# Tree feed-forward of an audio tower: four of eight levels weighed by ACT, residual added by GpSimd, one packed integer for four leaf numbers

## What is computed

```python
for _ in range(DEPTH + 1):                 # 8 levels, 255 nodes
    all_nodes.append(current)
    score = jnp.einsum('td,td->t', flat_x, w1s[current]) + b1s[current]
    all_logits.append(score)
    choice = ((jnp.sign(score) + 1.0) / 2.0).astype(jnp.int32)
    current = current * 2 + choice + 1
path_weights = jax.nn.gelu(jnp.abs(logits), approximate=False)
for i in range(DEPTH + 1):
    t_i = jnp.einsum('td,tdo->to', flat_x, w2s[nodes_i]) + b2s[nodes_i]
    out = out + t_i * path_weights[:, i][:, None]
...
h = h + _L0_ffn_ref(_layernorm(h, axis=-1), ...)
```

## Time and profile before

| | us |
|---|---|
| median of 3 runs (lowest to highest) | 495.93 (495.58 to 497.63) |
| the profiled execution | 497.14 |
| its span, first to last instruction | 495.4 |
| convolution, attention, sorting | 0 to 363 |
| static tiles, from the first gate | 367.6 |
| first overflow product | 420.45 |
| last product of the last overflow tile | 483.6 |
| last output DMA issued by GpSimd | 487.6 to 488.6 |

### The profile page before, as it was taken

One profiled execution on the slowest core, in us unless ns is written; L12 is line 12 of the kernel. 1 busy time (PEld: TensorE's weight loads), 2 busy tenths in 40 slices (PEclk: granted clock), 3 DMA queues, 4 the chain that ended last, 5 costly groups with the idle time before them and its releaser, 6 DMA issues.

```text
span 495.4 us, 8210 instructions
## 1 busy us (share of the span) xinstructions
PE 362.6 (73%) x2578; PEld 246.1 (50%) x2578; DVE 353.8 (71%) x619; ACT 297.0 (60%) x691; POOL 266.6 (54%) x354
## 2 busy tenths in 40 slices
PE   1158997767998897878987798834069887778880
PEld 1145665545555554456644475522057665545550
DVE  0558869897988888988889979776129999433341
ACT  1357987799789986777976658561013332544551
POOL 4324687885686846855896617417506555321111
PEclk9988989999999999898998989855569999999997
DMA  4443541339969722312441200197151220000000
GB/s 95 120 104 84 125 101 41 93 78 226 202 146 156 162 53 63 93 33 63 110 109 27 69 1 11 38 133 99 32 132 35 56 54 10 6 7 4 7 3 7
DMA packets 58424, 36.99 MB, mean 75 GB/s; under 512 B 31645, under 2 KB 57079, under 8 KB 58378
## 3 DMA queue, kind: packets, MB, share of 16 engines
q1 hardware_dynamic: 54250, 33.55, 33.6%
q0 software_dynamic: 3328, 2.36, 1.9%
q10 hardware_dynamic: 800, 0.49, 0.5%
HBM read 11.15 MB, written 7.50 MB: 38 GB/s over the span
## 4 chain that ended last, share of the span: by engine, by line
DVE 39%; PE 27%; ACT 15%; issue 11%; DMA 5%; POOL 1%; SPq 1%; DVEq 0%; POOLq 0%; ACTq 0%
DVE nm L1367 12%; ACT Z L1183 8%; PE Z L914 8%; DVE pre L1634 6%; PE Z L1051 5%; DVE va L1626 4%; DMA pre<-in_x 3%; DVE va L1396 2%; PE Z L1053 2%; ACT q L1125 2%; PE Z L1057 2%; DVE pre L1463 1%; ACT k L1125 1%; ACT va L1276 1%; PE Z L1055 1%
## 5 line engine op out<-in xcount | busy, mean ns | idle before, releaser
L1367 DVE TENSOR_REDUCE nm<-Z 125x1 f32<-125x748 f32 x192 | 175.4, 932 | 38.9 <-PE Z L914 33.2
L1183 ACT ACTIVATE Z<-Z,nm 125x748 f32<-125x748 f32 x192 | 166.1, 870 | 61.5 <-DVE nm L1367 61.2
L914 PE MATMUL Z<-pool_a 128*125 128x512 f16 (+1 forms) x768 | 164.5, 342 | 27.3 <-ACT Z L1183 23.7
L914 PEld LDWEIGHTS Z<-pool_a 128*125 128x125 f16 x768 | 88.7, 141 | 71.6 <-ACT Z L1183 45.6
L717 POOL DMA_INDIRECT out<-pre,va x44 | 42.7, 971 | 87.8 <-DVE pre L1640 78.3
L1634 DVE TENSOR_REDUCE pre<-va 128x64 f32<-128x512 f32 x44 | 45.1, 1025 | 1.3
L1276 ACT COPY va<-Z 32x520 f32<-32x520 f32 x48 | 27.9, 580 | 30.3 <-PE Z L1057 30.1
L781 PE MATMUL Z<-xhT,wq 128*128 128x249 f16 (+1 forms) x192 | 33.4, 295 | 10.5 <-DVEq L1377 9.2
L1183 ACT ACTIVATION_READ_ACCUMULATOR Z<-Z,nm 125x1 f32 x192 | 41.1, 214 | 0.0
L1051 PE MATMUL Z<-pool_a,qk 128*32 x96 | 29.6, 390 | 14.1 <-ACT va L1276 8.7
L646 POOL DMA_INDIRECT sorted_rows<-xrow,slot x24 | 30.4, 1266 | 15.3 <-DVE slot L1519 8.7
(11 more groups left out here) (237 smaller groups left out, 620.9 us busy)
## 6 DMA issues: line engine op xcount, KB each, us to landing
pool_a<-pool_a SPq DMA_DIRECT2D x64, 187.0 KB, 3.3
pool_a<-pool_a SPq DMA_DIRECT2D x64, 93.5 KB, 2.2
sorted_rows<-zrow SPq DMA_DIRECT2D x1, 3640.0 KB, 22.1
va<-sorted_rows SPq DMA_DIRECT2D x11, 260.0 KB, 3.4
w<-in_L_ffn_w2s SPq DMA_DIRECT2D x1, 2048.0 KB, 16.6
pre<-in_x SPq DMA_DIRECT2D x4, 375.0 KB
pool_a<-in_L_ffn_w2s SPq DMA_DIRECT2D x1, 1024.0 KB
out<-pre,va POOLq DMA_INDIRECT x44, 2.1
```

The source lines that it names most:

```text
L914: last = mm(z[0:XP, c0:c1], kst[:, u % 3, a, hd, KST[t]:KST[t] + XP], qst[:, u % 3, hd, c0:c1], start=(a == 0), stop=(a == 1))
L1183: sc_.activation(z, z, ACT.Exp, bias=nm[0:XP, u % 4, i:i + 1], accum_out=sm[0:XP, u % 4, i:i + 1]).then_inc(s_exp, 1)
L1367: v.tensor_reduce(nm[0:XP, u % 4, i:i + 1], Z[n % 3][0:XP, 0:N], X, ALU.max, negate=True).then_inc(s_max, 1)
```

## The change

Three edits, all in the feed-forward.

1. **Weighing.** In static tiles ACT weighs levels 0 to 3 (`AW = 4`), one instruction of 64 columns for each, with the level's gate as a scale for each row (`weigh_first`). DVE weighs levels 4 to 7 in one instruction of 256 columns. A new semaphore, "weighted_by_act", tells that ACT is done; PE's bank and DVE's sum wait for both. ACT's weighing of tile k waits until the sum of tile k - 2 has been made, since `wy` has two buffers. Overflow tiles are weighed as before.
2. **Residual.** DVE no longer adds it. GpSimd does, just ahead of the DMA in `rows_out`, for all tiles, and the DMA waits for it.
3. **Leaf numbers.** DVE packs four leaves of 7 bits in one integer (`lam4`), with two more instructions before "group_offsets". PE loads one integer a tile, after group 0 of the tile before, and for the first tile of a block ahead of the branch, so also for the blocks that are skipped. The node is cut out by one formula for all groups.

```diff
@@ def rows_out(k), GpSimd
+                pool.wait_ge(s_sl, k + 1)
+                o = yo[:, k % NO, :]
+                gp.tensor_tensor(o, o, xs[:, (k // 4) % NX, k % 4, C_H:C_ID], ALU.add).then_inc(s_yo, 1)
                 pool.wait_ge(s_yo, k + 1)
@@ def bank_ready(n), PE
                 elif n >= NY:
                     pe.wait_ge(s_wy, n - NY + 1)
+                    pe.wait_ge(s_wa, n - NY + 1)
@@ def load_leaves(k), PE
-                return [nc.tensor.value_load(lami[0:1, 2 * kk + i:2 * kk + i + 1], min_val=0,
-                                             max_val=LEAVES * LEAVES - 1) for i in range(2)]
+                return nc.tensor.value_load(lam4[0:1, kk:kk + 1], min_val=0, max_val=LEAVES ** 4 - 1)
@@ def overflow_products(k, leaves), PE
-                    if g % 2:
-                        return pairs[g // 2] >> (7 + sh)
-                    return (pairs[g // 2] >> sh) & (LEAVES - 1 >> sh)
+                    return (leaves >> (7 * g + sh)) & (LEAVES - 1 >> sh)
...
-                    if g == 2 and k % 4 < 3:
-                        following = load_leaves(k + 1)
...
+                    if g == 0 and k % 4 < 3:
+                        following = load_leaves(k + 1)
@@ blocks of overflow tiles, PE
+                leaves = load_leaves(4 * m)
                 with pe.If(groups > 4 * (4 * m - ST_TILES)):
                     xs_T(m)
-                    pairs = load_leaves(4 * m)
@@ static tiles, ACT
+            def weigh_first(k):
+
+                act.wait_ge(s_gelu, k + 1)
+                if k >= 2:
+                    act.wait_ge(s_sl, k - 1)
+                y = y_bank(k)
+                for n in range(AW):
+                    last = sc_.activation(wy[:, k % 2, n * D:(n + 1) * D], y[:, 0, n, 0:D], ACT.Copy,
+                                          scale=gw[:, k % 4, n:n + 1])
+                last.then_inc(s_wa, 1)
...
                 gates(k, y_bank(k))
+                weigh_first(k)
@@ leaf numbers, DVE
+            link(v.tensor_scalar(lam4[:], lami[:, 1::2], 14, None, ALU.logical_shift_left))
+            v.tensor_tensor(lam4[:], lam4[:], lami[:, 0::2], ALU.bitwise_or).then_inc(s_goff, 1)
@@ def weigh(k), DVE
+                y = y_bank(k)
+                v.tensor_tensor(w[:, 1], y[:, 1, :, 0:D], gv[:, 1], ALU.mult).then_inc(s_wy, 1)
@@ def sum_levels(k), DVE
+                if k < ST_TILES:
+                    dve.wait_ge(s_wa, k + 1)
...
-            def add_residual(k):
-                dve.wait_ge(s_sl, k + 1)
-                o = yo[:, k % NO, :]
-                v.tensor_tensor(o, o, xs[:, (k // 4) % NX, k % 4, C_H:C_ID], ALU.add).then_inc(s_yo, 1)
```

More of the change, by code:

```diff
@@ L163, in tower @@
         lami = sb("lami", [1, OVG // 2], i32)
+        lam4 = sb("lam4", [1, OVG // 4], i32)
         lamq = sb("lamq", [1, OVG], i32)
@@ L181, in tower @@
         NY = 3
+        AW = 4
         def y_bank(n):
@@ L214, in tower @@
             "slots", "ln2_rstd", "w1_columns")]
-        (s_b0, s_bnp, s_bn, s_bq8, s_z7, s_zl, s_abs, s_xp, s_xc, s_y, s_yv, s_wy, s_sl, s_yo) = [sem(n) for n in (
-            "b0_in", "bn_by_feature", "bn_ready", "q_bias_ready", "w7_zeros", "low_zeros", "gate_abs", "xs_T", "xsT_copied", "y_ready", "y_moved", "weighted", "levels_summed", "rows_out")]
+        (s_b0, s_bnp, s_bn, s_bq8, s_z7, s_zl, s_abs, s_xp, s_xc, s_y, s_yv, s_wa, s_wy, s_sl, s_yo) = [sem(n) for n in (
+            "b0_in", "bn_by_feature", "bn_ready", "q_bias_ready", "w7_zeros", "low_zeros", "gate_abs", "xs_T", "xsT_copied", "y_ready", "y_moved", "weighted_by_act", "weighted", "levels_summed", "rows_out")]
         vs, ps_, as_ = sem("vector_step"), sem("pool_step"), sem("scalar_step")
@@ L1029, in load_leaves, with overflow_products @@
                 kk = k - ST_TILES
-                return [nc.tensor.value_load(lami[0:1, 2 * kk + i:2 * kk + i + 1], min_val=0,
-                                             max_val=LEAVES * LEAVES - 1) for i in range(2)]
-            def overflow_products(k, pairs):
+                return nc.tensor.value_load(lam4[0:1, kk:kk + 1], min_val=0, max_val=LEAVES ** 4 - 1)
+            def overflow_products(k, leaves):
                 following = None
                 def node(g, sh):
-                    if g % 2:
-                        return pairs[g // 2] >> (7 + sh)
-                    return (pairs[g // 2] >> sh) & (LEAVES - 1 >> sh)
+                    return (leaves >> (7 * g + sh)) & (LEAVES - 1 >> sh)
                 tile_ready(k)
@@ L1068, in _ @@
             for m in range(ST_TILES // 4, F_TILES // 4):
+                leaves = load_leaves(4 * m)
                 with pe.If(groups > 4 * (4 * m - ST_TILES)):
                     xs_T(m)
-                    pairs = load_leaves(4 * m)
                     for k in range(4 * m, 4 * m + 4):
-                        pairs = overflow_products(k, pairs)
+                        leaves = overflow_products(k, leaves)
         @block.scalar
@@ L1618, in _ @@
             link(v.tensor_copy(lamf[:], lamq[:]))
-            v.scalar_tensor_tensor(lami[:], lamf[:, 1::2], float(LEAVES), lamf[:, 0::2], ALU.mult,
-                                   ALU.add).then_inc(s_goff, 1)
+            link(v.scalar_tensor_tensor(lami[:], lamf[:, 1::2], float(LEAVES), lamf[:, 0::2], ALU.mult, ALU.add))
+            link(v.tensor_scalar(lam4[:], lami[:, 1::2], 14, None, ALU.logical_shift_left))
+            v.tensor_tensor(lam4[:], lam4[:], lami[:, 0::2], ALU.bitwise_or).then_inc(s_goff, 1)
             def weigh(k):
                 dve.wait_ge(s_gelu, k + 1)
-                y = y_bank(k) if k < ST_TILES else yv[:, k % 2]
-                v.tensor_tensor(wy[:, k % 2].rearrange("p (h l o) -> p h l o", h=2, o=D), y[:, :, :, 0:D],
-                                gw[:, k % 4].rearrange("p (h l) -> p h l", h=2).unsqueeze(3).to_broadcast([P, 2, 4, D]),
-                                ALU.mult).then_inc(s_wy, 1)
+                w = wy[:, k % 2].rearrange("p (h l o) -> p h l o", h=2, o=D)
+                gv = gw[:, k % 4].rearrange("p (h l) -> p h l", h=2).unsqueeze(3).to_broadcast([P, 2, 4, D])
+                if k >= ST_TILES:
+                    v.tensor_tensor(w, yv[:, k % 2, :, :, 0:D], gv, ALU.mult).then_inc(s_wy, 1)
+                    return
+                y = y_bank(k)
+                v.tensor_tensor(w[:, 1], y[:, 1, :, 0:D], gv[:, 1], ALU.mult).then_inc(s_wy, 1)
             def sum_levels(k):
@@ L1654, in _ @@
                         sum_levels(k)
-                        add_residual(k)
 _INS = ["x", "L0_tok_kernel", "L0_tok_bias", "L0_tok_beta", "L0_tok_moving_mean", "L0_tok_moving_var",
```

3 lines of the change are left out of this document (removed).

## The result

| | before | after |
|---|---|---|
| median of 4 runs (lowest to highest) | 496.78 (495.58 to 504.49) | 508.03 (506.02 to 509.98) |
| the profiled execution, its span | 497.14, 495.4 | 506.02, 504.0 |
| last gate of the static tiles | 418.38 | 412.97 |
| first overflow product | 420.45 | 415.27 |
| first to last group of the three blocks | 18.74, 18.67, 18.62 | 22.14, 22.11, 22.15 |

The account below looks back on a forecast made before the run. The prediction took DVE to bound the static stage and PE's sequencer the even overflow groups. Terms -2.85 + 10.0 + 1.1 + 0.1 = +8.4 us, against 495.93, gave 504.3 us, range 494.0 to 509.5.

Parts of the forecast that it names:

- Static tiles: Static stage, timed by ACT's clock: first overflow product at 417.6 against 420.45, -2.85 us.
- the bound of -3.9: Static stage: with an ACT weighing step of 0.18, PE stays the limit and the gain is -3.9.
- GpSimd, +0.1 forecast: Residual add on GpSimd: 2.07 us a static tile, backlog some 8 tiles, about +0.1 at the very end.
- wait of DVE for the ring: Rival, end of static stage: GpSimd's tile takes 2.4 us, DVE waits for outputs, some 3 us; 507 us, chance 0.05.
- Overflow tiles, +10.0 forecast: Overflow blocks: register operations slow PE's sequencer, 22.0 us from first to last group; +3.3 a block, +10.0 in three.
- the lead of 0.03: Overflow tiles before: PE's sequencer is no more than 0.03 us ahead of the array when an even group begins.
- Borders, +1.1 forecast: Between overflow blocks: transposes wait for the hoisted load, +0.42 at each of two borders, +0.26 at the last.
- Loads of skipped blocks: End of execution: three loads run while DVE and GpSimd finish the last tile, costing nothing.
- The linear price for two operations: Rival, overflow tiles: two register operations cost 0.28, a group 1.12; 494.5 us, no difference, chance 0.13.
- The queue that hides the register work: Rival, overflow tiles: PE's sequencer gets far enough ahead or operations are cheap, array sets pace; 487.2 us, chance 0.07.
- ACT's weighing overlapped: Static tiles: steps overlap at 0.23 us; the rival without overlap had 0.33 a step, 516.1 us, chance 0.05.

Follow-up runs that it names:

- act_weighs_only: The kernel before with only ACT's weighing of four levels in the static tiles, residual still on DVE: ratio 0.9882 to the kernel before.
- odd_groups_masked: The kernel before with a mask added on the odd groups that changes no number: ratio 1.0374 to the kernel before, 518.6 us.
- mask_once: The changed kernel with each group's leaf cut out once and kept in a register: ratio 0.9643 to the kernel before, 481.10 us.
- packed_leaves_only: The kernel before with only the change's packed leaf numbers, masks and loads: ratio 1.0295 to the kernel before, 513.82 us.
- mask_once_residual_on_dve: mask_once with the residual back on DVE in all tiles: ratio 0.9609 to the kernel before, 479.54 us.

## Why the prediction held, step by step

**Static tiles, -2.85 forecast, -5.2 measured.** ACT's tile is 1.375 where I had 1.37. The measured gain lies beyond the bound of -3.9 that I gave, and three things were mis-sized in this term. I took PE's free pace of 1.47 a tile from two stretches of the earlier trace rows and added 0.03 a tile "with ACT, PE and DVE so close"; from the first gate (367.54) to the last the tiles average 1.465 us with their transposes, PE's own free pace, and nothing is lost between the engines: the last gate came at 412.97 instead of 414.5. 0.9 us of that is this addition. The other 0.6 is a balance: I put ACT's six copies of rows at 0.59 each, and a step with one takes 1.76, only 0.385 more than one without; against these 1.2 us stand 0.5 that ACT still waited for PE at the first tile and 0.005 a tile. And I charged ACT's register load with the 0.70 that it shows in the earlier trace rows, where its queue was empty; behind four queued weighings it is free (first overflow product 2.3 after the last gate, against my 3.1). Together 2.3 us in the change's favour. The last is the same rule that I had applied to PE, applied on one engine and forgotten on the other: a register load costs what the sequencer isn't ahead. The Trainium skill's figure from the page "VectorE: DVE Perf Modes" (section on the TRN2 errata) made a step of 0.20 and the trace has 0.20. My own 0.23 came from a rate of 1.4 elements a ns, which the rows come near to (gelu and copy in the earlier trace rows lie 504 elements and 0.37 us apart); the change from 249 elements to 64 took off 0.15 or 0.16 of the 0.36, not 0.13. The page's advice against small tiles spoke for a loss; cutting the weighing in four was a gain here, as ACT had the room.

**GpSimd, +0.1 forecast.** 2.13 a tile (2.07 forecast), no wait of DVE for the ring. From the last group to GpSimd's last transfer it is 5.42 us instead of 5.07, of which about 0.3 is the slower group itself: +0.1, as forecast, and hidden behind PE's end. It trailed DVE by ten tiles at the end of the stage, not eight, with a ring of twelve: the ring held nobody, but by less than I thought. What I had not seen is that the step was pointless (`act_weighs_only`).

**Overflow tiles, +10.0 forecast, +10.4 measured.** 22.1 us a block against 22.0, groups of 1.34 and a little more, 1.9 to 2.0 with a load. This was the step on which the forecast rested, and `odd_groups_masked` and `mask_once` show the cause from both sides. 0.4 us of each block was not worked out but added because the sum for the kernel before had missed it; it held. One sum on the way is wrong as written: 0.66 and 0.34 make 1.00, not 0.83. From the first product of an odd group to that of the next the sequencer has three products and that one to do, 0.50 + 0.335 = 0.83, and so the lead of 0.03 stands.

**Borders, +1.1 forecast.** Two at +0.48 (0.42 forecast), and the last group's +0.3.

**Loads of skipped blocks, "nothing" forecast: wrong.** +1.95 us behind the last product. I named DVE's and GpSimd's last tile as the cover, 5 us long, and never read what PE itself still had to do: three branches, 11.8 us. A cover has to be longer than what it covers, all of it. With this term right and the static term left, the forecast would have been 506.3; the miss in the static term hid it.

**Luck.** That +8.4 meets +8.6 is luck twice over: in the two errors, and in which executions were profiled. By the medians the forecast of 504.3 is 3.7 us low, within the range. No trace shows where the other executions spent the difference.

**The rivals.** The linear price for two operations (groups of 1.12) did not occur: at full clock 1.34 and more. The queue that hides the register work did not occur in the change, but did in `mask_once`: with six or seven register operations fewer a group the sequencer is ahead and hides most of a load. Its condition was right and its place was another kernel. ACT's weighing overlapped, and no wait of DVE for the ring shows.

## What to carry to other kernels

Where matmuls take their addresses from registers, count the register operations per product and compare the sequencer's time for a group with the array's; a value that several products share should be cut out once and kept. Work that moves off a bound engine frees only what stood in its chain: an addition in the shadow of a dependent pair is free where it is. And look at every engine's stream to its last instruction before calling something at the end hidden.

## What the runs showed of the hardware

**Skipping costs PE more than running.** A branch over a skipped block takes 2.7 to 4.8 us on PE (0.5 to 1.1 for the first of the three in the four kernels that cut the mask once and don't nest; why, isn't shown), whether one block or three are jumped over, and under 0.1 us into a block that runs. On GpSimd, ACT and DVE it takes 0.03 to 0.07 either way.

**GpSimd's closing drain** takes 6.3 to 6.8 us behind the last indirect DMA in every trace.

**The granted clock fell at the hand-over, where the static stage was faster.** The table by stretch of the changed kernel:

```profile
404.00:412.00 8.00, 8.00 (x97) 6.00 (x96) 7.50 (x12) 7.65 (x36) 4.71 (x9) 1.00 0.18 44
412.00:416.00 4.00, 2.25 (x23) 1.31 (x21) 3.73 (x6) 2.82 (x12) 2.53 (x4) 1.00 0.20 39
416.00:420.00 4.00, 3.34 (x17) 1.92 (x16) 0.07 (x1) 1.16 (x2) 2.62 (x4) 0.52 0.16 47
420.00:424.00 4.00, 4.00 (x25) 2.84 (x24) 0.15 (x1) 1.73 (x5) 2.63 (x4) 0.62 0.02 4
424.00:428.00 4.00, 3.89 (x28) 1.97 (x25) 1.57 (x2) 2.20 (x5) 2.47 (x4) 1.00 0.02 2
```

PE is busy without a gap to 412, then idle for 1.75 of 4 us, and then the clock stands at its lower level, 1.2 instead of 2.4 GHz, for most of 7 us. And in `packed_leaves_only`, whose static stage is that of before:

```profile
412.00:420.00 8.00, 6.50 (x79) 4.52 (x77) 8.00 (x15) 1.77 (x10) 4.78 (x5) 1.00 0.04 9
420.00:424.00 4.00, 2.14 (x14) 1.10 (x14) 4.00 (x8) 1.32 (x3) 2.00 (x3) 1.00 0.03 6
424.00:428.00 4.00, 3.84 (x25) 1.87 (x24) 0.72 (x2) 1.38 (x3) 1.94 (x2) 1.00 0.04 9
```

Of the nine profiles with ACT's weighing eight show such a dip within 10 us of the first overflow product; of the five without it, none, though PE idles as long there. Whether the busier stretch ahead is the cause isn't shown: the ninth, `mask_once_residual_on_dve`, is as busy and has no dip. Nor is ACT's weighing needed for a dip: `odd_groups_masked`, without it, has one at 488 to 491 us, in its third block, and the changed kernel has a second at 467 to 471. A dip costs little where the sequencer is the bound: in the first block of the changed kernel groups start up to 1.73 us apart at the lower clock, twice the array's 0.86, and then, with the sequencer ahead, follow after 1.20 and 1.06; the block takes 22.14, like the others. Where the array is the bound it shows: the first block took 15.1 to 15.5 us in the four profiles of kernels that cut the mask once and have the dip, and 14.4 to 14.5 in the two without it.
